# Expert results added to output rows by scattering transfers, in place of a slot store and a gather at the end

## The chip, the cores and the metric

The kernel runs on one core of a Trainium2 chip. The metric is device time in microseconds; the time before is the median of 3 runs, 1596.5 us (1591.99 to 1597.85). TensorE does the products, VectorE (DVE) and ScalarE (ACT) the elementwise work, GpSimd (POOL) elementwise work and the indirect DMAs, SyncE (SP) issues the plain DMAs.

## The reference

One layer on 1250 rows of 1024 features, in float32. Three parts follow one another: a graph convolution over 20000 edges and linear attention with 16 heads, both on the normalised rows and added to them, and then a mixture of 8 experts, 2 per row, whose result is added to the row:

```python
xn = _layernorm(x, axis=-1)
x = x + _L0_gnn_ref(xn, edge_index, L0_gnn_W, L0_gnn_b) + _L0_mix_ref(xn[None], ...)[0]
x = x + _L0_ffn_ref(_layernorm(x, axis=-1)[None], ...)[0]
...
logits = jnp.einsum('bsd,ed->bse', x, gate_w) + gate_b
topv, topi = jax.lax.top_k(logits, K)                       # K = 2 of E = 8
gate_score = jax.nn.softmax(where(keep > 0, logits, -inf))
expert_out = jnp.einsum('bsd,edo->bseo', x, expert_w) + expert_b
out = jnp.einsum('bseo,bse->bso', expert_out, gate_score)
```

## The kernel before

The change is in the third part and in the routing ahead of it. `x2` in SBUF holds the rows after the first two parts, ten tiles of 128 rows (TT = 10, the last of 98). Its normalised rows lie in DRAM in two halves of 512 columns, `x2n_half[c]`.

**Routing.** DVE finds the two best experts of each row (`choose`), makes the one-hot `both`, and TensorE counts rows per expert and ranks them (L1721 to L1726). DVE then works out for each row and choice its slot: every expert gets whole tiles of 128 slots, at least two, so that tile T of 128 slots belongs to one expert; `cnti` holds for each expert the number of tiles less one (`more`) and the first tile (`begin`). A product of `hotr` (which slot within a tile) and `hott` (which tile, times the row number), 20 matmuls (L1732), turns the table round: `slots[:, T]` is the row that each slot of tile T works on. The gate weights `gab` are worked out behind that, off any chain that waits for them (L1426 to L1435).

**Expert stage.** The tiles are worked through in order, in run-time loops (`experts`, `expert`, `tile_of`). For the given inputs these are 23 tiles, three to an expert and two for one. For tile T:

- POOL gathers its rows in two halves, `gather_tile`: a copy of the slot column to `here`, then an indirect DMA to `xg`.
- TensorE transposes a half (`transposes`, L1742), ACT makes the high part `mth` of it (`prepare`, L1054), DVE the low part `mtl` (`prepare`, L1391). This is done for tile T + 1 while tile T is multiplied: half 0 in the middle of tile T, half 1 at its end.
- TensorE multiplies in 48 matmuls of 512 columns (`tile`, L1756, L1757, L1759) in k order, k = 0 to 3 first, the transposes of the next tile, k = 4 to 7, the transposes again. Its results lie in one of two pairs of PSUM banks, by T odd or even, so `tile(T + 2)` waits for the copy of T.
- DVE adds the expert's bias `ebb` and copies to `ybuf` (`copy_out`, L1404), of which there is one, and SP stores it to its 128 slots in the DRAM tensor `slot_y` (`store_tile`, L590).

In the last tile of an expert ACT and DVE also split the next expert's weights into a high part (`high`, L1021) and a low part (L1419), k = 0 to 3 in the middle of the tile and k = 4 to 7 at its end; there `copy_out` comes behind those splits. SP loads the weights two experts ahead (`load_expert`, eight DMAs of 512 KB) once the last product of an expert is done, then stores that tile, then loads the next bias.

**Tail.** When all but the last expert's tiles are stored, POOL gathers for each of ten row tiles the result of its first choice (`gather_results`, L840), and when all tiles are stored those of the second. DVE multiplies each by its gate weight and adds it to `x2` (`combine`, L1444), and SP stores the finished row tiles to `out` (L615).

Engines run their own instruction streams, in the order written; everything between them goes by semaphores. SP's plain DMAs go through one queue, POOL's through another. To have no undefined numbers in slots that stay empty, SP fills `slot_y` with rows of x during attention (L527, 7 transfers).

Of the kernel before, what the change touches and what calls it, by code (L numbers as in the profile page):

```python
# [24 lines left out]
FILL = MAXT * P // (KT - 1)  # L25
assert FILL * (KT - 1) == MAXT * P and FILL <= NP
# [29 lines left out]
def gps_layer(nc, x, dst_pairs, src_cols, dst_cols, wg, bg, wq, bq, wk, bk, wv, bv, wo, bo, orf,  # L56
              gate_w, gate_b, expert_w, expert_b, out):
    x2n_half = [nc.dram_tensor(f"x2n_half{c}", [NP, CW], F32, kind="Internal").ap() for c in range(NC)]
    slot_y = nc.dram_tensor("slot_y", [MAXT * P, D], F32, kind="Internal").ap()
# [4 lines left out]
    with ctx:  # L64
# [49 lines left out]
        hott = keep("hott", [P, 2 * TT, MAXT], F32, s1)  # L114
# [103 lines left out]
        pc = ExitStack()  # L218
        gathered = keep("gathered", [P, 2 * KT, D], F32, pc)
        pc.close()  # L220
# [32 lines left out]
        pos = keep("pos", [P, 2, TT], I32)  # L253
        token = keep("token", [P, TT], F32)
# [5 lines left out]
        here = keep("here", [P, NC], I32)  # L260
        gw = keep("gw", [P, KT, E], F32)
# [107 lines left out]
        s_pos = sem("s_pos")  # L369
        slot_hot = sem("slot_hot")  # L370
        slots_filled = sem("slots_filled")
# [12 lines left out]
        y_stored = [sem(f"y_stored{c}") for c in range(NC)]  # L384
        z_stored = [sem(f"z_stored{c}") for c in range(NC)]
        a_gathered = sem("a_gathered")
        b_gathered = [sem(f"b_gathered{i}") for i in range(TT // 2)]
        comb_a = sem("comb_a")
        comb_b = sem("comb_b")
# [59 lines left out]
        def _(sp):  # L449
# [72 lines left out]
            with sp.Fori(1, KT) as j:  # L522
                for i, w in enumerate((wk, wv, wq)):

                    sp.wait_ge(a_w, START + 3 * j + i)
                    sp.dma_start(hraw[:, :, :], w[ds(j, 1)].rearrange("a p k n -> (a p) k n")).then_inc(a_raw, 16)
                sp.dma_start(slot_y[ds((j - 1) * FILL, FILL), :], x[0:FILL, :]).then_inc(slots_filled, 16)  # L527

# [57 lines left out]
            def store_tile(T, e, last):  # L586
                for c in range(NC):

                    sp.wait_ge(y_copied[c], T + 3)
                    sp.dma_start(slot_y[ds(T * P, P), c * CW:(c + 1) * CW],  # L590
                                 ybuf[:, c, :]).then_inc((z_stored if last else y_stored)[c], 16)

            def expert(e, par, last):
                more, begin = tiles(sp, e)
                with sp.Fori(0, more) as i:
                    store_tile(tile_of(begin + i), e, last)
# [5 lines left out]
                store_tile(T, e, last)  # L602
                if not last:

                    load_bias(e + 1)

            sp.wait_ge(slots_filled, 16 * (KT - 1))
            sp.wait_ge(s_cnti, 1)
            experts(sp, expert)


            for t in range(TT):
                n = LAST if t == TT - 1 else P
                sp.wait_ge(comb_b, t + 1)
                sp.dma_start(out[t * P:t * P + n, :], x2[0:n, t, :]).then_inc(s_out, 16)  # L615
# [4 lines left out]
        def _(pool):  # L620
# [31 lines left out]
            for signal in (rest_taken, rest_over, a_w, t_done, s_done, sq_ready, phi_done, kv_done, aux_done, kv_evac,  # L652
                           mt_trans, *y_stored, *z_stored):
# [128 lines left out]
            g.iota(token[:, :], [[P, TT]], base=0, channel_multiplier=1,  # L782
# [26 lines left out]
            def gather_tile(T):  # L809
                for c in range(NC):  # L810

                    pool.wait_ge(mt_trans, START + 2 * T - 1 + c if c else START + 2 * T - 1)
                    apart(pool)
                    g.tensor_copy(here[:, c:c + 1], slots[:, ds(T, 1)]).then_inc(here_ready, 1)
                    pool.wait_ge(here_ready, 2 * T + c + 1)
                    apart(pool)
                    g.indirect_dma_start(xg[:, c, :], None, x2n_half[c][:, :],
                                         bass.IndirectOffsetOnAxis(ap=here[:, c:c + 1], axis=0)).then_inc(xg_ready[c], 16)
# [24 lines left out]
            for t in range(TT):  # L843
                gather_results(t, 0, t, a_gathered)
# [984 lines left out]
```

## Time and profile before

| | |
|---|---|
| median of 3 runs | 1596.5 us |
| the profiled execution's own time | 1595.47 us |
| its span, first to last instruction | 1593.9 us |
| TensorE busy with matmuls | 1408.8 us (88%) |
| VectorE, ScalarE, GpSimd busy | 761.6, 465.5, 385.9 us |
| mean granted TensorE clock | 0.957 |

The span is that of one execution on the chip. A row of a timeline has the start, the duration, the engine (SPq is SyncE issuing), the line of the kernel, the operation and what it writes and reads, and in brackets how long the engine stood idle before it and what ended that. The busy share of an engine is a mean over stages with different limits, so a table by stage says more than the page's first lines.

### The profile page before, as it was taken

What the parts mean: (1) busy time and instruction counts of PE and PEld (TensorE: products, weight loads), DVE (VectorE), ACT (ScalarE), POOL (GpSimd) and SP (SyncE); (2) the same over time, 40 slices, a digit from 0 to 9 for tenths busy, and PEclk for the clock granted to TensorE, in tenths of its full rate; (3) what the DMA queues carried; (4) which work ended last, traced back from release to release, by engine and by line L of the source; (5) the groups of instructions that cost most, each with busy time, mean ns of one, the idle gap of its engine ahead of it and who ended that gap; (6) DMA issues with size and microseconds to landing.
All of it is one profiled execution on the core that took longest, in us unless ns stands there. A gap on an engine that the chain in (4) does not pass through costs nothing.

```text
span 1593.9 us, 26331 instructions
## 1 busy us (share of the span) xinstructions
PE 1408.8 (88%) x8396; PEld 1241.5 (78%) x8460; DVE 761.6 (48%) x1492; ACT 465.5 (29%) x777; POOL 385.9 (24%) x382
## 2 busy tenths in 40 slices
PE   5787778987889999999999999997999499999980
PEld 2465566887879999999999999996888388888860
DVE  7755443414354444444444444445454435444536
ACT  7412222401023232323333333332223023223310
POOL 7421443233230101010101010004034212122233
PEclk9999999998999999999999999998998599999995
DMA  4110111244321111111111101004234336665557
GB/s 152 52 36 17 60 46 71 73 134 127 96 87 73 39 67 37 69 40 66 40 66 43 63 33 59 1 1 140 77 128 145 126 96 239 237 237 201 215 205 280
DMA packets 64820, 158.19 MB, mean 99 GB/s; under 512 B 8010, under 2 KB 29210, under 8 KB 64320
## 3 DMA queue, kind: packets, MB, share of 16 engines
q1 hardware_dynamic: 55200, 127.20, 22.7%
q0 software_dynamic: 9568, 30.30, 6.1%
q8 instruction: 32, 0.52, 0.1%
q14 instruction: 20, 0.16, 0.0%
HBM read 120.05 MB, written 55.78 MB: 110 GB/s over the span
## 4 chain that ended last, share of the span: by engine, by line
PE 74%; DMA 8%; DVE 6%; issue 5%; POOL 2%; ACT 2%; DVEq 2%; SPq 1%; POOLq 0%; ACTq 0%
PE PB L1579 6%; PE PB L1581 6%; PE PB L1580 6%; DMA y_scratch<-xrow 5%; PE PB L1756 5%; PE PB L1757 5%; PE PB L1759 5%; PE PB L1615 5%; PE PB L1638 4%; PE PB L1481 4%; PE PB L1563 2%; PE PB L1565 2%; PE PB L1564 2%; PE PB L1522 2%; PE PB L1523 2%
## 5 line engine op out<-in xcount | busy, mean ns | idle before, releaser
L1579 PE MATMUL PB<-xh,hw 128*128 128x416 f32 (+1 forms) x576 | 205.0, 356 | 5.5 <-ACT qf L966 5.5
L1581 PE MATMUL PB<-xh,hw 128*128 128x416 f32 (+1 forms) x576 | 203.0, 352 | 0.0
L1580 PE MATMUL PB<-xl,hw 128*128 128x416 f32 (+1 forms) x576 | 202.8, 352 | 0.0
L1756 PE MATMUL PB<-mwh,mth 128*128 128x512 f32 x368 | 149.0, 405 | 1.3 <-issue 1.3
L1481 PE MATMUL PB<-ohs,ohd 128*128 x471 | 105.8, 346 | 48.8 <-DVE ohs L1127 32.6
L1757 PE MATMUL PB<-mwl,mth 128*128 128x512 f32 x368 | 144.5, 393 | 0.0
L705 POOL CAST hw<-hraw 128x1024 fp32r<-128x1024 f32 x24 | 24.9, 1037 | 455.5 <-PE PB L1581 450.7
L1481 PEld LDWEIGHTS PB<-ohs,ohd 128*128 x534 | 51.7, 97 | 101.5 <-issue 84.4
L1550 PE MATMUL PB<-hh,AT 128*128 128x256 f32 x400 | 103.7, 298 | 18.2 <-DVE hr L1141 9.2
L1579 PEld LDWEIGHTS PB<-xh,hw 128*128 128x128 f32 x576 | 108.6, 189 | 7.6 <-ACT qf L966 6.5
L1125 DVE TENSOR_SCALAR ohd<-iota,dc 128x128 f16 x178 | 60.0, 337 | 113.9 <-PE PB L1481 101.7
L1759 PE MATMUL PB<-mwh,mtl 128*128 128x512 f32 x368 | 114.2, 392 | 0.0
L1580 PEld LDWEIGHTS PB<-xl,hw 128*128 128x128 f32 x576 | 108.7, 189 | 1.2
L1581 PEld LDWEIGHTS PB<-xh,hw 128*128 128x128 f32 x576 | 108.6, 189 | 1.2
L1127 DVE TENSOR_SCALAR ohs<-iota,sc 128x1280 f16 x178 | 101.8, 572 | 0.0
L1551 PE MATMUL PB<-hr,AT 128*128 128x256 f32 x400 | 101.2, 292 | 0.0
L1550 PEld LDWEIGHTS PB<-hh,AT 128*128 128x128 f32 x400 | 80.5, 201 | 21.3 <-DVE xrow L1178 10.4
L1054 ACT ACTIVATE mth<-PB 128x512 fp32r<-128x512 f32 x48 | 28.7, 598 | 226.2 <-PE PB L1742 226.2
L1522 PE MATMUL PB<-wqh,xh 128*128 128x256 f32 x320 | 91.7, 287 | 3.1 <-DVE xl L1134 1.7
L1391 DVE TENSOR_TENSOR mtl<-PB,mth 128x512 fp32r<-128x512 f32 x48 | 33.0, 688 | 126.6 <-ACT mth L1054 126.6
L966 ACT ACTIVATE qf<-PB,biasT 128x416 f32<-128x416 f32 (+1 forms) x48 | 29.2, 609 | 216.3 <-PE PB L1581 167.2
L1523 PE MATMUL PB<-wql,xh 128*128 128x256 f32 x320 | 90.5, 283 | 0.0
(261 smaller groups left out, 3147.7 us busy)
## 6 DMA issues: line engine op xcount, KB each, us to landing
mraw<-expert_w SPq DMA_DIRECT2D x64, 512.0 KB, 7.5
slot_y<-x SPq DMA_DIRECT2D x7, 2560.0 KB, 12.1
slot_y<-ybuf SPq DMA_DIRECT2D x46, 256.0 KB, 3.4
count_rests<-ATf POOLq DMA_DIRECT2D x9, 640.0 KB, 3.3
xrow<-x SPq DMA_DIRECT2D x40, 128.0 KB, 2.4
y_scratch<-xrow SPq DMA_DIRECT2D x40, 128.0 KB, 2.4
yrow<-y_scratch SPq DMA_DIRECT2D x20, 256.0 KB, 2.9
x2n_half<-xhat SPq DMA_DIRECT2D x20, 256.0 KB, 2.5
```

What stands on the lines that cost most here:

```text
L1127: v.tensor_scalar(ohs[:, ds(2 * side + p, 1), :].rearrange("p a n -> p (a n)"), iota[:, :], sc[:, ds(col, 1)], None, ALU.is_equal).then_in ...
L1481: ins = mm(PB[:, 1536 * s + c0:1536 * s + c0 + n], ohd[:, ds(2 * side + p, 1), :].rearrange("p a n -> p (a n)"), ohs[:, ds(2 * side + p, 1 ...
L1522: mm(o, xh[:, k, at], wqh[q % 2][:, k, :], start=(k == 0), stop=False)
L1523: mm(o, xh[:, k, at], wql[q % 2][:, k, :], start=False, stop=False)
L1550: mm(o, AT[:, b, at], hh[:, q % 2, b, :], start=(b == 0), stop=False)
L1551: ins = mm(o, AT[:, b, at], hr[:, q % 2, b, :], start=False, stop=(b == TT - 1))
L1579: mm(bank(i, n), hw[:, wi, 0, k, :], xh[:, k, c0:c0 + n], start=(k == 0), stop=False)
L1580: mm(bank(i, n), hw[:, wi, 0, k, :], xl[:, k, c0:c0 + n], start=False, stop=False)
L1581: ins = mm(bank(i, n), hw[:, wi, 1, k, :], xh[:, k, c0:c0 + n], start=False, stop=(k == KT - 1))
L1756: mm(y[c], mth[:, k, :], mwh[par][:, k, c * CW:(c + 1) * CW], start=(k == 0), stop=False)
L1757: mm(y[c], mth[:, k, :], mwl[par][:, k, c * CW:(c + 1) * CW], start=False, stop=False)
L1759: ins = mm(y[c], mtl[:, k, :], mwh[par][:, k, c * CW:(c + 1) * CW], start=False, stop=(k == KT - 1))
```

## The change

The result of an expert tile is no longer stored by slots. At the start of the expert stage SP writes `x2` to `out`. For each tile DVE copies the products with the bias to `ybuf` as before, ACT multiplies both halves by the gate weight of each slot (`scale`), and POOL adds the 128 rows to their rows of `out` with one indirect DMA that accumulates in DRAM (`add_tile`); empty slots aim beyond the last row and are left out by the bounds check. `copy_out` of the next tile waits until that transfer has landed, which POOL waits for half a tile later (`tile_added`) and tells by `y_free`; the last one is awaited by SP. For this, routing turns two tables round instead of one: the slot's row number (for the gather, `slots`, and for the scatter, `target`) and its gate weight (`gate`), so `hott` is twice as wide and `gab` is worked out earlier, ahead of DVE's wait for TensorE's counts. In the last tile of an expert `copy_out` and `scale` stand ahead of the splits for k = 4 to 7; the last tile of all has no `prepare` behind it any more. `slot_y`, its fills, the gathers and the combines at the end are gone, and the stores of `out` are at the start.

```diff
+            for t in range(TT):
+                n = LAST if t == TT - 1 else P
+                sp.dma_start(out[t * P:t * P + n, :], x2[0:n, t, :]).then_inc(s_out, 16)
...
             def expert(e, par, last):
                 more, begin = tiles(sp, e)
-                with sp.Fori(0, more) as i:
-                    store_tile(tile_of(begin + i), e, last)
                 T = tile_of(begin + more)
                 if not (isinstance(e, int) and e >= E - 2):
                     sp.wait_ge(prod_done, T + 1)
                     load_expert(e + 2, par)
-                store_tile(T, e, last)
                 if not last:
+                    for c in range(NC):
+                        sp.wait_ge(y_copied[c], T + 3)
                     load_bias(e + 1)
...
+            more, begin = tiles(sp, E - 1)
+            sp.wait_ge(y_added, 16 * (begin + more + 1))
             sp.wait_ge(s_out, 16 * TT)
```

On POOL (`gather_half(T, c)` is one half of the old `gather_tile(T)`):

```diff
+            def aim(T):
+                g.tensor_copy(there[:, :], target[:, ds(T, 1)]).then_inc(there_ready, 1)
+            def add_tile(T):
+                pool.wait_ge(y_scaled, NC * (T + 1))
+                pool.wait_ge(there_ready, T + 1)
+                g.indirect_dma_start(out[:, :], bass.IndirectOffsetOnAxis(ap=there[:, 0:1], axis=0),
+                                     ybuf[:, :, :].rearrange("p c n -> p (c n)"), None, bounds_check=N - 1,
+                                     oob_is_err=False, compute_op=ALU.add).then_inc(y_added, 16)
+            def tile_added(T):
+                pool.wait_ge(y_added, 16 * (T + 1))
+                pool.sem_inc(y_free, 1)
+                aim(tile_of(T + 1))
...
-            with pool.Fori(0, begin + more + 1) as T:
-                gather_tile(tile_of(T + 1))
...
+            gather_half(1, 0)
+            gather_half(1, 1)
+            pool.wait_ge(targets_ready, 1)
+            aim(0)
+            gather_half(2, 0)
+            gather_half(2, 1)
+            pool.wait_ge(s_out, 16 * TT)
+            add_tile(0)
+            with pool.Fori(2, begin + more + 1) as T:
+                gather_half(tile_of(T + 1), 0)
+                tile_added(tile_of(T - 2))
+                gather_half(tile_of(T + 1), 1)
+                add_tile(tile_of(T - 1))
+            tile_added(tile_of(begin + more - 1))
+            add_tile(tile_of(begin + more))
```

On ACT and DVE:

```diff
+            def scale(T):
+                for c in range(NC):
+                    act.wait_ge(y_copied[c], T + 3)
+                    a.mul(ybuf[:, c, :], ybuf[:, c, :], gate[:, ds(T, 1)]).then_inc(y_scaled, 1)
             def expert(e, par, last):
                 with act.Fori(0, more) as i:
                     for h in range(2):
                         prepare(begin + i + 1, h)
-                for h in range(2):
-                    prepare(begin + more + 1, h)
-                    if not last:
+                    scale(tile_of(begin + i))
+                if not last:
+                    for h in range(2):
+                        prepare(begin + more + 1, h)
+                        if h == 1:
+                            scale(tile_of(begin + more))
                         for k in range(4 * h, 4 * h + 4):
                             high(e + 1, k, 1 - par)
+                else:
+                    scale(tile_of(begin + more))
...
             v.tensor_tensor(both[:, :, :], oneh[:, 0], oneh[:, 1], ALU.add).then_inc(s_both, 1)
+            dve.wait_ge(s_ge, 1)
+            link(v.tensor_scalar(gd[:, 3, :], gd[:, 1, :], 1.0, None, ALU.add))
...
             dve.wait_ge(route_done, 1)
...
-            for i in range(2):
-                v.tensor_tensor(hott[:, i * TT:(i + 1) * TT, :], hota[:, i * TT:(i + 1) * TT, :], token..., ALU.mult)
+            for i, value in enumerate((token[:, :], gab[:, 0, :, :].rearrange("p i t -> p (i t)"))):
+                v.tensor_tensor(hott[:, :, i, :], hota[:, :, :], along(value, MAXT), ALU.mult).then_inc(slot_hot, 1)
...
-                    if last:
-                        dve.wait_ge(y_stored[c], START + 16 * begin)
-                        dve.wait_ge(z_stored[c], START + 16 * i)
-                    else:
-                        dve.wait_ge(y_stored[c], START + 16 * T)
+                    dve.wait_ge(y_free, T + START)
...
-            v.tensor_copy(slots[:, :], bank(2, MAXT)).then_inc(slots_ready, 1)
+            v.tensor_scalar(slots[:, :], found[:, 0:MAXT], float(FAR), float(N - 1), ALU.add, ALU.min).then_inc(slots_ready, 1)
+            v.tensor_copy(gate[:, :], found[:, MAXT:2 * MAXT])
+            v.tensor_scalar(target[:, :], found[:, 0:MAXT], float(FAR), None, ALU.add).then_inc(targets_ready, 1)
```

On TensorE only the slot product changes, from `hott[0:n, i, :]` of MAXT = 35 columns to both tables, 70 columns.

## Rows read from the trace of the kernel before

**Rows 1.** Table by stage: busy of each engine, then PEclk, DMA share, GB/s.

```profile
1236.00:1269.00 33.00, 12.12 (x56) 11.79 (x55) 16.97 (x57) 0.21 (x1) 6.62 (x6) 0.50 0.37 136
1269.00:1547.70 278.70, 276.97 (x1296) 228.08 (x1296) 122.78 (x147) 81.17 (x103) 62.38 (x100) 0.99 0.56 197
```

**Rows 2.** Timeline of the tail: start, duration, engine, line, operation.

```profile
1546.69 0.62 PE L1759 MATMUL PB<-mwh,mtl 128*128 128x512 f32 x2
1549.10 1.28 DVE L1404 TENSOR_TENSOR ybuf<-PB,ebb 128x512 f32<-128x512 f32 x2
...
1558.55 1.18 POOL L840 DMA_INDIRECT gathered<-slot_y,pos  x1 [8.10 <-DMA slot_y<-ybuf]
...
1571.07 19.70 SPq L615 DMA_DIRECT2D out<-x  x10
```

**Rows 3.** Timeline of one tile within an expert.

```profile
1298.95 0.60 ACT L1054 ACTIVATE mth<-PB 128x512 fp32r<-128x512 f32 x1 [5.33 <-PE PB L1742]
...
1299.97 0.97 POOL L817 DMA_INDIRECT xg<-x2n_half,here  x1 [0.79 <-POOL here L814]
...
1304.15 0.60 PE L1742 MATMUL PB<-ident,xg 128*128 128x128 f32 x4
```

**Rows 4.** Landing times of transfers from `resty` (L726) and then to `gathered` (L840).

```profile
DMA to landing us min/median/max: 3.1/3.5/3.9
...
DMA to landing us min/median/max: 4.6/6.7/11.9
```

**Rows 5.** DMA queues and issues, windows 445.3:450, 319.9:324, 324:330, 1266:1270.5.

```profile
q0 software_dynamic: 288, 0.20, 33.0%
...
q0 software_dynamic: 144, 0.07, 8.8%
...
q1 hardware_dynamic: 576, 0.52, 27.6%
...
q0 software_dynamic: 160, 0.52, 41.8%
...
xg<-x2n_half,here POOLq DMA_INDIRECT x2, 3.5
```

**Rows 6.** Timeline of the routing stage, DVE and POOL.

```profile
1243.31 0.24 DVE L1350 COPY tot<-PB 128x80 f32<-128x80 f32 x1 [1.97 <-PE PB L1725]
...
1254.86 0.95 DVE L1385 TENSOR_TENSOR hott<-hota,token 128x350 f32<-128x350 f32 x2
...
1264.76 0.16 DVE L1427 TENSOR_SCALAR gd<-gd 128x10 f32<-128x10 f32 x1
...
1265.52 1.16 POOL L828 DMA_INDIRECT xg<-x2n_half,here  x1 [0.29 <-POOL here L825]
...
1266.86 0.17 DVE L1435 TENSOR_TENSOR gab<-gab 128x10 f32<-128x10 f32 x1
```

**Rows 7.** Groups by line and shape: busy us, mean ns of one, idle before.

```profile
L1732 PE MATMUL PB<-hott,hotr 128*128 128x35 f32 x36 | 8.1, 408 | 12.6 <-DVE hott L1385 12.6
...
L1724 PE MATMUL PB<-both,upper 128*128 128x72 f32 x2 | 0.7, 456 | 3.9 <-DVE both L1347 3.9
```

**Rows 8.** What the DMA engines moved in 1236:1265, in 40 slices.

```profile
GB/s 0 113 282 350 418 418 396 401 441 407 418 429 396 429 390 401 96 0 0 0 0 0 0 0 0 0 0 0 0 0 0 0 0 0 0 0 0 0 0 0
```

**Rows 9.** Timeline of a boundary of two experts, and the late bias.

```profile
1311.29 3.90 ACT L1021 ACTIVATE mwh<-mraw 128x1024 fp32r<-128x1024 f32 x4
1311.43 0.69 DVE L1391 TENSOR_TENSOR mtl<-PB,mth 128x512 fp32r<-128x512 f32 x1 [0.35 <-ACT mth L1054]
...
1312.38 4.63 DVE L1419 TENSOR_TENSOR mwl<-mraw,mwh 128x1024 fp32r<-128x1024 f32 x4 [0.26 <-ACT mwh L1021]
...
1316.01 0.60 PE L1742 MATMUL PB<-ident,xg 128*128 128x128 f32 x4
...
1328.32 1.29 DVE L1404 TENSOR_TENSOR ybuf<-PB,ebb 128x512 f32<-128x512 f32 x2 [4.34 <-DMA ebb<-expert_b]
```

**Rows 10.** Landing of xg in the window 1310:1330, with eight weight loads.

```profile
xg<-x2n_half,here POOLq DMA_INDIRECT x4, 5.9
```

More of the change, by code:

```diff
@@ L24 @@
 MAXT = (2 * N + 2 * (P - 1)) // P + 1 + 2 * (E - 2) + 1
-FILL = MAXT * P // (KT - 1)
-assert FILL * (KT - 1) == MAXT * P and FILL <= NP
+FAR = 4096
 CHUNKS = ((0, 512), (512, 512), (1024, NP - 1024))
@@ L260, in gps_layer @@
         here = keep("here", [P, NC], I32)
+        target = keep("target", [P, MAXT], I32)
+        there = keep("there", [P, 1], I32)
+        gate = keep("gate", [P, MAXT], F32)
         gw = keep("gw", [P, KT, E], F32)
@@ L383, in gps_layer @@
         y_copied = [sem(f"y_copied{c}") for c in range(NC)]
[L384 to L389, printed above, removed]
+        targets_ready = sem("targets_ready")
+        y_scaled = sem("y_scaled")
+        there_ready = sem("there_ready")
+        y_added = sem("y_added")
+        y_free = sem("y_free")
         s_out = sem("s_out")
@@ L807, in _, with gather_half @@
                 low(k)
[L809 to L818, printed above, removed]
+            def gather_half(T, c):
+                pool.wait_ge(mt_trans, START + 2 * T - 1 + c if c else START + 2 * T - 1)
+                apart(pool)
+                g.tensor_copy(here[:, c:c + 1], slots[:, ds(T, 1)]).then_inc(here_ready, 1)
+                pool.wait_ge(here_ready, 2 * T + c + 1)
+                apart(pool)
+                g.indirect_dma_start(xg[:, c, :], None, x2n_half[c][:, :],
+                                     bass.IndirectOffsetOnAxis(ap=here[:, c:c + 1], axis=0)).then_inc(xg_ready[c], 16)
             pool.wait_ge(slots_ready, 1)
@@ L829, in _ @@
                                      bass.IndirectOffsetOnAxis(ap=here[:, c:c + 1], axis=0)).then_inc(xg_ready[c], 16)
-            more, begin = tiles(pool, E - 1)
-            with pool.Fori(0, begin + more + 1) as T:
-                gather_tile(tile_of(T + 1))
-            for c in range(NC):
-                pool.wait_ge(y_stored[c], START + 16 * begin)
-                apart(pool)
-            def gather_results(t, i, at, done):
-                n = LAST if t == TT - 1 else P
-                g.indirect_dma_start(gathered[0:n, at, :], None, slot_y[:, :],
-                                     bass.IndirectOffsetOnAxis(ap=pos[0:n, i, t:t + 1], axis=0)).then_inc(done, 16)
@@ L843, in _ @@
[L843 to L854 removed]
+            def aim(T):
+                apart(pool)
+                g.tensor_copy(there[:, :], target[:, ds(T, 1)]).then_inc(there_ready, 1)
@@ L1392, in prepare, with copy_out @@
                                 mth[:, 4 * h:4 * h + 4, :].bitcast(F32), ALU.subtract).then_inc(mt_low, 1)
-            def copy_out(T, e, i, begin, last):
+            def copy_out(T, e):
                 for c in range(NC):
@@ L1411, in expert @@
                         prepare(begin + i + 1, h)
-                    copy_out(begin + i, e, i, begin, last)
-                for h in range(2):
-                    prepare(begin + more + 1, h)
-                    if not last:
+                    copy_out(begin + i, e)
+                if not last:
+                    for h in range(2):
+                        prepare(begin + more + 1, h)
+                        if h == 1:
+                            copy_out(begin + more, e)
                         for k in range(4 * h, 4 * h + 4):
```

77 lines of the change are left out of this document (20 added, 57 removed).

## Prediction

> **What bounds the kernel now.** I read the page first, for the order of the stages, then the table by stage, then the timelines where one stage turns into the next. The table puts numbers on it: from 1269 to 1547.7 us TensorE works 277.0 of 278.7 us at a granted clock of 0.99 (the 2.4 GHz level), while the 33 us of routing ahead of it run at 0.50 (1.2 GHz) with TensorE busy for 12 [rows 1]. The last product ends at 1546.69 + 0.62 = 1547.3 and the span at 1593.9, so 46.6 us hold no product at all [rows 2]. Three stages count, each with its own limit: routing is a chain of small DVE and TensorE steps, the expert stage is TensorE alone, the tail is transfers. What the change does in a stage has to be read against that stage's limit.
>
> **What goes: the tail.** After the last product come a copy, a store, ten gathers that waited 8.1 us for that store, combines behind the gathers, and ten output stores issued from 1571.07 to 1590.8 [rows 2]. All of that is replaced.
>
> **What comes in its place.** The last copy_out no longer stands behind a prepare, so its two halves (1.28 us [rows 2]) run from 1547.35 to 1548.65. ScalarE then scales the second half: no such instruction is in the trace; the nearest is the 128x512 ACTIVATE at 0.60 [rows 3]; end 1549.25. POOL waits and issues: the shortest gap ahead of an indirect issue is 0.29 [rows 6], the one behind a copy and its wait is 0.79 [rows 3]; I take 0.5, issue at 1549.75. Then the scattering transfer, X us from issue to landing, and 0.3 (a gap of that kind) until the span closes. The end is 1550.05 + X.
>
> **X, which the trace doesn't show.** From below: a gather of the same 128 rows of 4 KB landed in 4.6 at the quickest. The only accumulating transfers are the four of 128 KB in 1 KB rows, which landed in 3.1 to 3.9 [rows 4]. The queue shares tell what they cost the DMA engines. Queue 0 held 33.0% of 16 engines over 4.7 us (24.8 engine-us) for one such transfer and the load of restb in front of it; a load of restb alone held 8.8% over 4.1 us (5.8). That leaves 19.0 for 128 rows, 0.148 each. Plain 1 KB rows: 27.6% over 6 us is 26.5 for 512 rows, 0.052 each [rows 5]. An accumulated row costs 0.10 more, or 2.85 times as much. A gathered 4 KB of xg costs 41.8% of 4.5 us, 30.1 for 128, 0.235; eight rows per engine are then 2.65 us with the constant added and 5.4 with the factor. An xg gather of 3.5 us has 0.94 of data, so 2.6 of fixed time [rows 5], and X is 5.25 by the first and 8.0 by the second. The bounds are 4.6 and 8.0. I take 6.0, nearer to the additive reading, since the quick landings of 3.1 to 3.9 are mostly fixed time.
>
> By the Trainium skill, Collectives: The Full Stack, "The bandwidth ceiling: the fold count and why AG ≠ RS ≠ AR", an add in a DMA engine reads two sources for each write and so runs at half the rate of a copy. By that the data part is 3.8 (twice two xg gathers), X is 6.4, and the sum below would be 0.4 later. The trace's 1 KB rows are worse than a factor of two.
>
> The stage ends at 1556.05 if nothing ahead of it moves: 37.85 saved.
>
> **Routing, on the path.** Eleven small DVE links (1264.76 to 1267.03, 2.3 us) move between `both` and the wait for TensorE's counts. That wait was 1.97 long [rows 6] and ScalarE's exp comes before it, so 0.35 shows (bounds 0 and 2.3). The two `hott` products, 0.95 together [rows 6], double their columns: +0.8 (0.7 to 0.95); `pos` goes, less than 0.1, left out. The 40 slot matmuls get 70 columns for 35. At this same low clock 72 columns take 0.456 and 35 take 0.408, 48 ns [rows 7]; as those ends are modelled I take 0.03 each, 1.2 (bounds 0 and 1.9). Sum +2.35, less what `pos` gave: 2.25. The copies for `gate` and `target` come after slots_ready, under the first gather; POOL's `aim` lies ahead of a wait for TensorE.
>
> **Ten stores of x2 to out, earlier.** SyncE issues them behind expert 1's eight loads. Those moved at about 400 GB/s and were over at 1248 [rows 8]; 5.1 MB more at that rate end at 1261, and the first xg gather is issued at 1265.5 [rows 6]. Free; without that cover the first gather is late by some us. POOL's wait for them stands before add_tile(0), with gather_half(3, 0) behind it, all long after.
>
> **slot_y fills.** Seven transfers from DRAM to DRAM during attention go. POOL and TensorE wait for none of them: 0; a gain is excluded by TensorE's products bounding that stage.
>
> **Each tile in the expert stage.** A tile takes 11.86 us (transposes at 1304.15 and 1316.01 [rows 3, 9]). ybuf is single, and its ring is now copy 1.28, scale 0.6, POOL 0.5, X, release 0.3: 2.7 + X, 8.7 for X = 6. It fits while X is under 9.15. tile_added has the second gather_half queued behind it on POOL, whose rows TensorE wants a tile later; the wait on y_free has prepare of the next tile behind it on DVE, wanted at the end of that tile. ScalarE's 1.2 us more per tile lie in idle of 5.33 [rows 3]. All hidden under TensorE's products, and uncovered from 9.15 on.
>
> **The boundary of two experts** (seven). copy_out and scale move ahead of the weight splits for k = 4 to 7. Before: mtl ends at 1312.12, then four highs in 3.90 and four lows in 4.63. After: copies to 1313.4, scale to 1314.05, first high to 1315.1, first low (1.2) to 1316.3; TensorE wants it right after the transposes of 1316.01, at 1316.35 [rows 9]. The margin is nil. I charge 0.15 each, 1 us. SyncE asks for the bias sooner, no store being ahead of it, but behind the same 4.2 MB of loads, and the scatter takes more of the DMA engines than the store did; ebb arrived at 1328.3 [rows 9] and I leave it there.
>
> **Sum.** 1593.9 - 37.85 + 2.25 + 1.0 = 1559.3 of span; 1.57 us lie outside the span (1595.47 - 1593.9), so 1560.9. The profiled execution was 1.0 under the median of the runs, 1596.5. I predict 1561.5. Bounds: X -1.4 to +2, routing -1.5 to +2.9, boundaries -1 to +7: 1557.5 to 1573.5.
>
> **Rivals.** (1) *The boundaries stall.* While eight loads run, an xg gather lands in 5.9 instead of 3.5 [rows 5, 10]. A scatter of 8 undisturbed is then slower still, and takes 4 us more of the engines than the store did, so the bias comes later too. Worked out for the worst: first copy of an expert 1331, its scatter lands 1341.5; second copy 1342, landing 1352.5; the last tile's copy is wanted at 1347.7 and highs and lows wait behind it: 5 us at the six boundaries that follow a burst, 30, so 1590; a middle case is 1575. For it: the nil margin. Against it: with X = 6 the ring recovers within a tile. Chance 0.17.
>
> The Trainium skill, DMA: Bandwidth & Descriptors, "Queues, rings and completion order", has each engine take turns between the queues with work, packet by packet. The landings of xg in the burst agree. By that rule a scatter of 6 takes 9.4 there, just past the ring, and one of 8 takes 13.4, which is the worst case.
>
> (2) *The scatter is the bound: slower.* One mechanism: read, add and write of 4 KB rows take longer than a tile leaves. Each us of X above 9.15 costs 22 us over 23 tiles. At X = 10.7 the gain is gone, from 11.1 the kernel is slower by over 0.5%, and X = 12 gives 1561.5 + 22 x 2.85 = 1624. For it: the factor of 2.85, and gathers and loads on the same engines. Against it: even the factor gives 8.0 undisturbed. Chance 0.10.
>
> (3) *The x2 stores reach into the first gather, or an indirect issue blocks on POOL while its queue is full*: the gain shrinks by 10 to 25 us, 1572 to 1586. Chance 0.08.
>
> The forecast holds the remaining 0.65. Range: 1555 to 1584. A measurement of this kernel tells about 0.5% (8 us) from nothing. Faster by more 0.87, within it 0.04, slower 0.09.
>
> **What the new profile would show.** The last scatter landing in 5 to 8 us and the span ending 8 to 11 us after the last product; slots at 1266 to 1268; slot matmuls near 10 us; TensorE idle in the expert stage at most 5 us more, tiles still 11.86 apart; the stores of x2 over before the first xg. I am wrong if DVE waits for y_free at every tile, or TensorE for mwl at the boundaries.

## The result, and the profile after

The changed kernel took 1572.8 us (median of four runs, 1569.7 to 1575.4) against 1595.2 for the kernel before on the same chip: a ratio of 0.986, 95% interval 0.9832 to 0.9887. The forecast was 1561.5, within 1555 to 1584. The gain is real and 11 us smaller than forecast. The profiled execution (1575.38, span 1573.8) stands beside the 1593.9 of before, 20.1 us less. The same table by stage as [rows 1], with the tail as a third window:

```profile
1236.00:1271.20 35.20, 14.13 (x64) 13.74 (x64) 17.16 (x58) 1.92 (x3) 7.40 (x7) 0.50 0.73 274
1271.20:1560.80 289.60, 281.08 (x1296) 230.03 (x1296) 124.02 (x147) 108.25 (x146) 105.66 (x137) 0.98 0.61 177
1560.80:1573.80 13.00, 0.00 (x0) 0.00 (x0) 1.07 (x2) 1.33 (x2) 1.62 (x1) 0.64 0.11 16
```

TensorE's last product now ends 13.4 us before the span does, where it was 46.6 [rows 2]. But the expert stage, 278.7 us long before, is 289.6 for the same 1296 instructions. A good part of what the tail gave was lost there.

**The tail**, in the timeline of all engines, and below it SyncE's and GpSimd's closing instructions (the last two columns of each are nanoseconds and the first and last start):

```profile
1559.74 0.62 PE L1750 MATMUL PB<-mwh,mtl 128*128 128x512 f32 x2
...
1560.58 1.29 DVE L1412 TENSOR_TENSOR ybuf<-PB,ebb 128x512 f32<-128x512 f32 x2 [9.00 <-PE PB L1750]
1561.47 1.33 ACT L1055 ACTIVATE ybuf<-ybuf,gate 128x512 f32<-128x512 f32 x2 [8.94 <-DVE ybuf L1412]
1563.93 1.62 POOL L823 DMA_INDIRECT out<-ybuf,there  x1 [3.39 <-issue]
```
```profile
L62 POOLq DRAIN  x1: 9912/9912/9912, 1563.7 to 1563.7; - x1
L62 SPq COMPARE_BRANCH  x1: 38/38/38, 1569.9 to 1569.9; - x1
```

SyncE is released at 1569.9, so the last scatter landed 5.9 us after its issue; the forecast had 6.0. The agreement is partly luck: this scatter moved 0.21 MB, since most slots of the last tile are empty (the one before it, 0.52 MB, landed in 6.6), and the others outside a burst of weight loads landed in 6.0 to 6.6. GpSimd's closing drain, which begins with that issue, ends at 1563.7 + 9.9 = 1573.6, and the span with it.

**The expert stage.** The transposes that end each half of a tile were 5.93 us apart before (1280.44 to 1547.14 in 45 steps). I call what is over 45 such steps (266.7 us) the losses. The third transposes and the last ones now:

```profile
1283.59 0.60 PE L1733 MATMUL PB<-ident,xg 128*128 128x128 f32 x4
...
1560.20 0.60 PE L1733 MATMUL PB<-ident,xg 128*128 128x128 f32 x4
```

1560.20 - 1283.59 - 266.7 = 9.9 us of losses, where before had none. They are not spread evenly: five places, each near a boundary of experts, hold 9.2 of them (1.7, 0.7, 1.4, then 3.9 and 1.5 about the expert of two tiles). The waits that go with them, from the list of waits (engine, tile and line, what released it: us in all, times, the longest):

```profile
POOL there L816 <- DMA out<-ybuf,there: 72.6, 22, 5.7
...
DVE ybuf L1412 <- DMA ebb<-expert_b: 25.2, 6, 5.4
...
DVE ybuf L1412 <- POOLq L830: 14.2, 9, 3.1
...
PE PB L1733 <- DMA xg<-x2n_half,here: 8.6, 3, 4.6
...
PE PB L1747 <- DVE mwl L1429: 2.8, 3, 1.3
```

DVE's wait for the bias is nearly as large as before, when it was 29.0 us in six. New are the nine waits for y_free (released by POOLq L830). Of TensorE's 8.6 us for xg, 4.8 lie ahead of the first tile's products (bias_pair, which loses next to nothing, has them too), and one wait of 3.8 is in the stage. Its three waits "for mwl" need care, since the list names the releaser that came last before the wait ended. The first of these places is in the timeline:

```profile
1332.64 1.29 DVE L1412 TENSOR_TENSOR ybuf<-PB,ebb 128x512 f32<-128x512 f32 x2 [5.36 <-DMA ebb<-expert_b]
...
1335.81 1.61 POOL L823 DMA_INDIRECT out<-ybuf,there  x1 [5.25 <-ACT ybuf L1055]
...
1342.21 0.18 POOL L816 COPY there<-target 128x1 int32 x1 [2.81 <-DMA out<-ybuf,there]
...
1343.32 0.96 POOL L801 DMA_INDIRECT xg<-x2n_half,here  x1 [0.79 <-POOL here L798]
...
1345.42 1.62 POOL L823 DMA_INDIRECT out<-ybuf,there  x1 [1.14 <-ACT ybuf L1055]
...
1345.93 4.63 DVE L1429 TENSOR_TENSOR mwl<-mraw,mwh 128x1024 fp32r<-128x1024 f32 x4 [0.26 <-ACT mwh L1015]
...
1348.95 0.60 PE L1733 MATMUL PB<-ident,xg 128*128 128x128 f32 x4
...
1350.80 0.49 PE L1747 MATMUL PB<-mwh,mth 128*128 128x512 f32 x1 [1.25 <-DVE mwl L1429]
```

The list's reading, late splits for k = 0 to 3, doesn't fit. The product at 1350.80 needs the low part for k = 0 alone, the first of the four, and that ended at 1345.93 + 1.23 = 1347.16; the 1350.56 that the list goes by is the end of the fourth. What fits is TensorE's own instruction stream. At the start of an expert it reads the expert's number of tiles and first tile from `cnti` in SBUF (L395, L396), as it does in every kernel here; the column PEldq is its sequencer, the numbers are nanoseconds (min/median/max). These are the two reads at this place, then all eight of L396 in the changed kernel and in bias_pair:

```profile
L395 PEldq TENSOR_LOAD <-cnti x1: 596/596/596, 1347.5 to 1347.5; - x1
L396 PEldq TENSOR_LOAD <-cnti x1: 1147/1147/1147, 1348.6 to 1348.6; - x1
...
L396 PEldq TENSOR_LOAD <-cnti x8: 297/722/1535, 1273.8 to 1522.9; - x8
...
L396 PEldq TENSOR_LOAD <-cnti x8: 296/302/309, 1274.2 to 1514.2; - x8
```

So read it as this chain. The bias of the new expert lands behind eight weight loads, so the expert's first copy_out runs at 1332.64. Its scatter is issued at 1335.81 and holds ybuf for 6.4 us. The second tile's copy_out waits until 1342.24. GpSimd too waits for that landing, until 1342.21, so the gather_half behind it is issued at 1343.32 and lands at 1346.57. TensorE's stream, which otherwise runs ahead of its products, waits for that xg and comes to the two reads at 1347.47, 1.5 us ahead of the transposes, where bias_pair has 2.4. There they meet the next late scatter (issued at 1345.42) and take 0.60 and 1.15 us instead of 0.30 each. The second ends at 1349.72 and the product starts 1.08 later, where it would have followed the transposes at 1349.30. At the two other places (0.7 and 1.4 us) the product starts 1.13 and 1.12 us after the second read too, and 3.4 and 3.6 us after the low part that it needs. The three together are 3.7 us.

About the expert of two tiles the late scatter (1480.64) stands directly in front of a gather_half, and TensorE waits for its xg:

```profile
1480.64 1.61 POOL L823 DMA_INDIRECT out<-ybuf,there  x1 [5.37 <-ACT ybuf L1055]
1481.67 1.88 POOL L798 COPY here<-slots 128x1 int32 x1
1484.34 1.20 POOL L801 DMA_INDIRECT xg<-x2n_half,here  x1 [0.79 <-POOL here L798]
...
1493.12 1.09 PE L1733 MATMUL PB<-ident,xg 128*128 128x128 f32 x4 [3.77 <-DMA xg<-x2n_half,here]
```

In bias_pair that gather is issued 4.1 us ahead of the previous transposes, here 1.1 us behind them, and it lands in 8.5 us, with the next eight weight loads issued from 1483.61 on. The 1.5 us that follow are TensorE's clock. After these 3.8 us without products the granted clock was 0.50 (the 1.2 GHz level) for 3.4 us, and a product took 0.63 us for 0.39:

```profile
1493.00:1496.20 3.20, 3.08 (x10) 2.63 (x11) 2.65 (x3) 0.81 (x2) 0.96 (x2) 0.50 1.03 334
```

The same kernel's other trace, changed_again, has its 9.0 us in part elsewhere: 4.1 at the same three places and 0.9 by two waits for xg at others, but 1.65 and 1.58 where the low part for k = 4 does come too late, since the tile's copy_out ahead of it had waited for y_free:

```profile
1490.99 3.50 DVE L1429 TENSOR_TENSOR mwl<-mraw,mwh 128x1024 fp32r<-128x1024 f32 x3 [1.92 <-ACT mwh L1015]
...
1492.36 0.47 PE L1747 MATMUL PB<-mwh,mth 128*128 128x512 f32 x1 [1.41 <-DVE mwl L1429]
```

Its first low part ends at 1492.22. So a late scatter is common to all these places, and by which way it reaches TensorE changes from place to place and from run to run.

**Routing** cost less than forecast. From the timeline of DVE and the groups by shape:

```profile
1244.85 0.24 DVE L1365 COPY tot<-PB 128x80 f32<-128x80 f32 x1
...
1256.32 0.89 DVE L1399 TENSOR_TENSOR hott<-hota,token 128x700 f32<-128x700 f32 x1
1257.12 0.88 DVE L1399 TENSOR_TENSOR hott<-hota,gab 128x700 f32<-128x700 f32 x1
```
```profile
L1722 PE MATMUL PB<-hott,hotr 128*128 128x70 f32 x36 | 8.2, 423 | 13.5 <-DVE hott L1399 13.5
```

The eleven links moved `tot` 0.25 us back (2.46 us behind the start of `both`, 2.21 before). The x2 stores, with expert 1's loads, filled the DMA engines until about 1262, and the first xg was issued at 1267.8. They cost nothing.

### The profile page after: what moved, and what is told of

Same layout as the page of the kernel before. It is cut to its first block, busy times and chain, and to the rows that moved or that the text cites. A ratio compares the mean times of both kernels' runs of the same rounds, so it can differ in the third digit from the quotient of the medians.

```text
span 1573.8 us, 26445 instructions
## 1 busy us (share of the span) xinstructions
PE 1428.5 (91%) x8459; PEld 1245.6 (79%) x8460; DVE 735.5 (47%) x1471; ACT 493.4 (31%) x821; POOL 411.1 (26%) x408
## 3 DMA queue, kind: packets, MB, share of 16 engines
q1 hardware_dynamic: 48016, 96.79, 17.8%
## 4 chain that ended last, share of the span: by engine, by line
PE 72%; DMA 12%; DVE 5%; issue 5%; ACT 2%; SPq 2%; POOL 1%; DVEq 0%; POOLq 0%; ACTq 0%
PE PB L1569 7%; PE PB L1571 7%; PE PB L1570 7%; PE PB L1471 6%; DMA y_scratch<-xrow 6%; PE PB L1605 5%; PE PB L1628 4%; PE PB L1747 4%; PE PB L1748 3%; PE PB L1750 3%; DMA ebb<-expert_b 2%; PE PB L1553 2%; PE PB L1555 2%; PE PB L1554 2%; PE PB L1512 2%
## 5 line engine op out<-in xcount | busy, mean ns | idle before, releaser
L1471 PE MATMUL PB<-ohs,ohd 128*128 x534 | 120.3, 352 | 36.9 <-issue 23.3
L1130 DVE TENSOR_SCALAR ohd<-iota,dc 128x128 f16 x178 | 55.1, 309 | 115.4 <-PE PB L1471 104.7
L1132 DVE TENSOR_SCALAR ohs<-iota,sc 128x1280 f16 x178 | 106.8, 600 | 0.0
L1514 PE MATMUL PB<-wqh,xl 128*128 128x256 f32 x320 | 90.5, 283 | 0.0
L1747 PEld LDWEIGHTS PB<-mwh,mth 128*128 128x128 f32 x368 | 70.3, 191 | 19.2 <-issue 5.5
```

Of the source, the lines that this page charges most:

```text
L1132: v.tensor_scalar(ohs[:, ds(2 * side + p, 1), :].rearrange("p a n -> p (a n)"), iota[:, :], sc[:, ds(col, 1)], None, ALU.is_equal).then_in ...
L1471: ins = mm(PB[:, 1536 * s + c0:1536 * s + c0 + n], ohd[:, ds(2 * side + p, 1), :].rearrange("p a n -> p (a n)"), ohs[:, ds(2 * side + p, 1 ...
L1747: mm(y[c], mth[:, k, :], mwh[par][:, k, c * CW:(c + 1) * CW], start=(k == 0), stop=False)
```

## The experiments

Theory A for the losses changed on the way. In the first expectations (bias_pair, copy_behind_splits, scatter_without_add) it is the late bias that costs, and the ring of ybuf only hands the delay on. After their results it has two conditions: the bias is late, *and* the single ybuf is held until its slow, adding scatter lands. The main rivals, by the letters of the expectations below: the scatter alone is too slow (B of bias_pair), the late bias alone is enough (D of scale_on_gpsimd), the place of the copies costs (C) or doesn't matter at all (G), or GpSimd has too much to do (E of scale_on_gpsimd). The letters B, D and E stand for other things in other expectations. The table has all runs; "losses" and "tail" (from the start of the weight loads of the last transposes to the end of the span) are worked out from the traces in one way for all.

```
run                             time us   ratio (95%)              losses  tail
before                          1595 to 1598                        0.0    47.0
the changed kernel              1572.8    0.986  (0.983 to 0.989)    9.9    13.8
changed_again                   1576.4    0.988  (0.986 to 0.990)    9.0    14.1
bias_pair                       1564.6    0.980  (0.977 to 0.983)    1.4    14.6
bias_pair_again                 1567.0    0.981  (0.979 to 0.984)    1.4    14.3
bias_ahead_of_weights           1568.6    0.982  (0.979 to 0.985)    2.0    14.1
scatter_without_add (1 run)     1560.8                               1.7    12.5
copy_behind_splits              1575.3    0.987  (0.984 to 0.990)    9.5    14.4
bias_pair_copy_behind_splits    1573.3    0.986  (0.983 to 0.988)   11.8    14.4
scale_on_gpsimd                 1616.6    1.014  (1.010 to 1.017)   46.2    20.5
scale_on_gpsimd_bias_pair       1618.2    1.013  (1.009 to 1.016)   48.3    21.1
last_by_plain_store (1 run)     1568.9                               9.1     7.8
gpsimd_waits_for_last_landing   1570.7    0.984  (0.982 to 0.986)    1.4    17.8
```

**bias_pair.** The bias of an expert is loaded two experts ahead, into one of two buffers (and the semaphores of biases and raw weights are split by parity).

```diff
-        ebb = keep("ebb", [P, D], F32)
+        ebb = keep("ebb", [P, 2, D], F32)
...
-            load_bias(0)
+            load_bias(0, 0)
+            load_bias(1, 1)
...
-                if not last:
...
-                    load_bias(e + 1)
+                    load_bias(e + 2, par)
```

> Edit: two bias buffers, the bias of an expert loaded two experts ahead (and semaphores for weights and bias kept apart by parity); nothing else. In the changed kernel VectorE waited 25.2 us in all for ebb, 14.2 for y_free, and TensorE lost 9.9 us against an even 5.93 us per half tile. Theory A (the late bias starts the delays, the ring of ybuf only hands them on): waits for ebb below 2 us, waits for y_free below 5, TensorE's losses below 3, time about 8 us less, 1565. Rival B (the scattering transfer is too slow for the ring by itself while the weights load): waits for ebb gone, but 10 us and more for y_free, losses of 6 to 9, time 1570 or more.

Losses fell from 9.9 to 1.4 us, with no wait for ebb left and 5.8 us for y_free (just over the 5 expected), and so the scatter alone (B) is not enough:

```profile
  PE PB L1750: 9.0, 1
  POOLq L830: 5.8, 5
```

The stretch of the expert stage, with TensorE busy for 279.0 of 280.9 us, is within 2.2 us of what it was in [rows 1]:

```profile
1271.60:1552.50 280.90, 279.00 (x1296) 228.83 (x1296) 123.30 (x147) 109.25 (x146) 103.22 (x137) 0.98 0.63 181
```

**bias_ahead_of_weights.** One buffer, but SyncE issues the bias first (the semaphores of the raw weights are split by parity as in bias_pair).

```diff
                     sp.wait_ge(prod_done, T + 1)
-                    load_expert(e + 2, par)
+                    apart(sp)
                 if not last:
...
                     load_bias(e + 1)
+                if not (isinstance(e, int) and e >= E - 2):
+                    load_expert(e + 2, par)
```

> SyncE issues the next expert's bias ahead of the eight 512 KB weight loads instead of behind them; the buffer stays single. SyncE therefore also waits for the tile's two copies (y_copied) before it issues the weights. Theory A (the bias is late because it queues behind eight weight loads, and the late copy is what the single ybuf and its scatter turn into a TensorE wait): ebb lands in 3 to 5 us instead of 13.6, DVE waits for ebb fall from 25.2 to below 5, waits for y_free from 14.2 to about the 5.8 of the run with the pair of biases, expert-stage losses below 3 us, time 1563 to 1568. Rival B (the weights, issued some 2 us later, become late instead): ACT's splits wait for mraw, losses stay, time 1570 or more.

No wait for ebb is left, y_free 8.8 us, losses 2.0. Its time, 1568.6, is just over the range given. Rival B of this run falls: the weights, asked for later, were not missed. The order of two requests on SyncE's queue is worth about 8 of the 9.9 us.

**scatter_without_add.** The scatter overwrites its rows instead of adding to them, so the sum over a token's two experts and its x2 is left out. The bias stays late.

```diff
-                                     oob_is_err=False, compute_op=ALU.add).then_inc(y_added, 16)
+                                     oob_is_err=False).then_inc(y_added, 16)
```

> Leaves out the addition: the scattering transfers overwrite the rows of out instead of adding to them, all else the same. It prices the add. The adding transfer landed in 6.5 us (median) and took 46.4% of 7.6 us of 16 engines, 56.4 engine-us for 128 rows, 0.44 each. Additive theory: a plain scattered row costs 0.10 less than an adding one, landing 5.9. Factor theory: a plain row costs a half or less, 0.15 to 0.22, landing 4.6 to 5.1. TensorE's losses: by theory A still 6 or more, because the bias stays behind 4.2 MB of loads; by rival B below 4.

Theory A missed here: it gave losses of 6 or more, and they are 1.7. DVE waits for the bias as long as ever, so the late bias alone, as A had it first and D has it later, is not enough. The buffer comes free sooner:

```profile
DVE ybuf L1412 <- DMA ebb<-expert_b: 25.3, 6, 5.2
```
```profile
1330.73 1.01 POOL L823 DMA_INDIRECT out<-ybuf,there  x1 [6.50 <-ACT ybuf L1055]
...
1334.40 0.19 POOL L816 COPY there<-target 128x1 int32 x1 [0.69 <-DMA out<-ybuf,there]
1334.43 1.29 DVE L1412 TENSOR_TENSOR ybuf<-PB,ebb 128x512 f32<-128x512 f32 x2 [0.26 <-POOLq L830]
```

The hold is 3.7 us instead of 6.4, and the waits for y_free fall from 14.2 us to 0.3. So neither condition costs by itself, and both together cost about 8 us. That the second condition is the hold of ybuf is argued, not shown: the edit takes more away than that. The scatter also takes less of the DMA engines, GpSimd issues it in 1.0 us for 1.6, and 15 of TensorE's 16 reads of `cnti` take 0.30 to 0.32 us, the other 0.58. (Of the 14.5 us by which its span is shorter than the changed kernel's, 8.2 are losses and 1.3 the tail. 3.5 were there before its first transposes and 1.5 come from its first tile at the low clock; in both the edit has no part.)

**copy_behind_splits** and **bias_pair_copy_behind_splits.** copy_out and scale of an expert's last tile stand behind all eight weight splits, as copy_out did before, with the single bias and with the pair.

```diff
                     for h in range(2):
                         prepare(begin + more + 1, h)
-                        if h == 1:
-                            copy_out(begin + more, e)
...
+                copy_out(begin + more, e)
```

> Edit: at the boundary of two experts copy_out and scale stand behind the weight splits for k = 4 to 7 again, as in the kernel before. My forecast saw the danger in that order (nil margin, 0.15 us each). If it is that, the small losses in the second half of the first tile after a boundary (0.17, 0.17, 0.36 us and the like) vanish and the time falls by 1 us. Theory A: the big losses (1.7, 0.7, 1.4, 3.9, 1.5) stay, since they come from the first tile's late bias; total 8 to 12, time 1571 to 1576. Rival C (the order is what costs): losses below 5, time 1568 or less.

> The pair of biases, and the tile's copy and scaling behind the eight weight splits, as the kernel before had them. Theory A (the late scatter, whatever makes it late, costs through ybuf and through GpSimd's gather queued behind it): the copies wait for y_free about 40 us in all as in the run with the copy behind the splits and the single bias, expert-stage losses 8 to 10 us, time 1571 to 1576, so moving the copies ahead of the last four splits is worth 7 to 10 us once the bias is there in time. Rival G (the place of the copies does not matter, only the bias does): 1563 to 1567.

Alone it changes nothing in the time, and that theory A's figure (8 to 12 us of losses) came out was luck. A gave them to the late bias, but the bias is then rarely waited for (4.7 us), while y_free is, 40.9 us in all. The copies come late because they stand behind the splits, and each late scatter reaches the next. TensorE loses most of it otherwise too, by six waits for xg of 6.5 us in all. With the pair it is 8.6 us slower than the pair alone, and DVE waits 44.7 us for y_free (of its losses 1.6 stand in 3.4 us at a granted clock of 0.50, from 1336.1 on). So the scatters about a boundary must be early, and two things make them late: the place of the last tile's copy and the bias of the next expert's first. Either spoils what curing the other would give, which is why the move in the changed kernel by itself showed no gain. Rivals C and G fall.

**scale_on_gpsimd** and **scale_on_gpsimd_bias_pair.** DVE's copy goes to a buffer of its own and GpSimd multiplies by the gate into ybuf; this was meant to take the hold of the scatter off DVE.

```diff
+                for c in range(NC):
+                    pool.wait_ge(y_copied[c], T + 3)
+                    g.tensor_scalar(ybuf[:, c, :], ypre[:, c * CW:(c + 1) * CW], gnow[:, 0:1], None,
+                                    ALU.mult).then_inc(y_scaled, 1)
```

> GpSimd multiplies by the gate just before its scatter, from a buffer of its own that DVE fills, so DVE's copy no longer waits for a landing and ScalarE no longer scales; the bias keeps its single buffer and its place. Theory A (two conditions together cost the 9.9 us: a late bias and a single result buffer held until the scatter lands): waits for y_free are gone, ebb waits stay near 25, expert-stage losses below 3 us as in the run without the addition (1.7), tail about 1 us longer by two GpSimd products of 0.5 to 1 us each in place of ScalarE's; time 1565 to 1569. Rival D (it is the late bias alone that costs, by holding DVE in front of the splits): losses stay 8 to 10, time 1573 or more. Rival E (GpSimd, now with 2 more us a tile, issues the gathers late): TensorE waits for xg, over 1575.

> Both at once: GpSimd scales from a buffer of its own, and the biases have a pair of buffers. Theory A: the losses were already down to 1.4 us with the pair of biases alone, so nothing more is to be had in the expert stage; the tail is up to 1 us longer; time 1564 to 1567, the same as with the pair alone (1564.6). Rival F (the five waits for y_free of 5.8 us that the pair of biases left still cost): 1561 to 1563.

Both miss theory A by some 50 us. Rival E holds, and I had underpriced it. A product took 1.7 us on GpSimd where ScalarE took 0.7, and a round of GpSimd (two products, scatter, landing, two gathers) passes a tile's 11.86 us: here 14.2 from one copy of `there` to the next, 1301.22 to 1315.40.

```profile
1301.22 0.18 POOL L819 COPY there<-target 128x1 int32 x1 [3.02 <-DMA out<-ybuf,there]
...
1303.42 3.15 POOL L828 TENSOR_SCALAR ybuf<-x,gnow 128x512 f32<-128x512 f32 x2
1307.49 2.69 POOL L832 DMA_INDIRECT out<-ybuf,there  x1 [0.91 <-POOL ybuf L828]
...
1315.40 1.20 POOL L819 COPY there<-target 128x1 int32 x1 [2.43 <-DMA out<-ybuf,there]
```

After the first tile TensorE waited 31.4 and 36.6 us for xg. As tests of theory A these two are void, since another engine became the bound. A pair of ybufs with everything else alike, which would test the hold itself, was not tried.

**last_by_plain_store.** The last tile's scatter is left out; SyncE stores its ybuf to the first rows of out in its place.

> Leaves out the last scatter: the last tile's scaled result goes to rows 0 to 127 of out by one plain store of SyncE. It asks what ends the span. In the changed kernel the last scatter landed 5.9 us after its issue, and the span ended 3.7 us later, with GpSimd's closing drain. Theory D (the drain ends 3.7 us after the last of GpSimd's own transfers has landed): the scatter before landed 0.1 us after the last product, so the drain ends 4 us after it, the store at about 6; the span ends 6 to 7 us after the last transposes begin instead of 13.6. Rival E (the drain takes about 10 us from where GpSimd's stream ends, whatever is in flight): 10 to 11 us after them.

The tail shrank by 6.0 us, to 7.8. The store was issued at 1562.44, SyncE was released at 1565.1 and the span ended 2.2 us later, with GpSimd's drain, although GpSimd had nothing outstanding:

```profile
L62 POOLq DRAIN  x1: 7427/7427/7427, 1559.7 to 1559.7; - x1
```

Both theories of this expectation miss. D had the drain end 3.7 us after the scatter before had landed (1559.56), and it took 7.4; E had about 10. The tail, 7.8, lies between the two.

**gpsimd_waits_for_last_landing.** bias_pair, and GpSimd waits for its own last landing before it ends.

```diff
             add_tile(tile_of(begin + more))
+            pool.wait_ge(y_added, 16 * (begin + more + 1))
```

> The kernel with the pair of biases, in which GpSimd itself waits for the landing of its last scatter before it comes to its end. In the runs so far GpSimd's closing drain began when the last scatter was issued and ended 3.7 us after that scatter landed; where the last tile left by SyncE (last_by_plain_store), GpSimd had already waited for everything and its drain still took 7.4 us. Theory H (a closing drain of GpSimd takes 7.4 us from its start and at least 3.7 us from the last landing, so the end of the program is GpSimd's whoever waits for the landing): the drain begins at the landing, takes 7.4 us, and the span ends some 18 us after the last transposes instead of 14.6; time about 1568, 3 to 4 us more than the 1564.6 of the pair alone. Rival I (the 3.7 us are only the last transfer's bookkeeping, done once it has landed): the drain takes 3.7 us or less from the landing and the time stays at 1563 to 1566.

```profile
L62 POOLq DRAIN  x1: 7059/7059/7059, 1559.6 to 1559.6; - x1
```

The drain began at the landing and took 7.1 us; the tail grew from 14.6 to 17.8. Theory H holds in the trace. The time, 1570.7, is 2.7 over what it gave (the ratio is 0.4 points above bias_pair's, some 7 us, of which the tail explains 3.3; the rest I can't place, as it isn't in this trace).

**bias_pair_again** and **changed_again**, five rounds each on one chip.

> The same kernel as bias_pair, timed in five rounds beside the changed kernel on one chip. Expected from the traces: 8 to 9 us below the changed kernel (expert-stage losses of 1.4 us in place of 9.9), ratio to the kernel before near 0.980.

> The changed kernel itself, unaltered, on the same chip as bias_pair_again: ratio to the kernel before near 0.986, and in its trace again waits of DVE for ebb near 25 us, for y_free near 14 us, and losses of 8 to 11 us in the expert stage.

9.4 us apart, with losses of 1.4 and 9.0 and waits for y_free of 6.1 and 17.7 us. The version with the pair of biases beats both kernels: 1.9% below before and 0.6% below the change, and its interval (0.979 to 0.984) lies clear of the change's (0.986 to 0.990).

## Why the prediction was right, and where it was off

The sum gave a span of 1559.3; it was 1573.8. By terms:

- **Tail, -37.85 forecast, -33.2 measured.** The mechanism was right, and X came out (5.9 for 6.0) on a last tile that is mostly empty. The step that failed is the last one, "0.3 until the span closes": it took 3.9, from GpSimd's drain (+3.6). The gap ahead of the issue was 1.13 for my 0.5, and scale ended 0.5 later, since ScalarE takes 0.7 a half and waits for each. Before, GpSimd's drain took 16.7 us and ended at 1591.4, 3.7 after its last gather had landed, and SyncE waited for the output stores until 1593.5, which hid it; the change took that cover away. I had read SyncE's end of the program as the program's end.
- **Boundaries, +1 forecast, +9.9 measured.** The largest miss. "Against it: with X = 6 the ring recovers within a tile" is the step that failed: the ring recovers, but only by delaying what stands behind it, GpSimd's next gather and DVE's next splits, and those have too little slack in an expert of three tiles. It was rival 1 (chance 0.17), at a third of the worst case's price and near its middle case (1575), to which the measured 1572.8 is nearer than to the 1561.5 forecast. But rival 1 had only its chain by the splits for k = 4 to 7. In the changed kernel's first trace that way cost some 0.6 us; the rest went by the gathers: 3.7 by TensorE's reads of `cnti`, 3.9 by the wait for xg, 1.5 by the low clock after it. In changed_again rival 1's own way took 3.2 of 9.0. The nil margin alone, on which I had charged the 1 us, cost 0.16 to 0.34 at each of the seven boundaries in bias_pair, 1.4 in all. Of the signs of being wrong, TensorE's wait for mwl at the boundaries came true in changed_again, and DVE waited for y_free in nine of 23 tiles.
- **Routing, +2.25 forecast, +0.3 measured** (1237.60 to 1264.65 before, 1239.56 to 1266.90 now). The 70 columns cost the slot matmuls 423 ns for 408, some 0.6 us over 40, and their stretch 0.1; the eleven links cost 0.25 for the 0.35 forecast; `hott` took 1.77 for 0.95, as forecast, and the first gd subtraction happened to take 0.7 less.
- **Free, as forecast:** the x2 stores, the slot_y fills, ScalarE's scaling inside an expert.
- **Not the change's:** +1.96 stood ahead of the routing stage, and +0.9 in the first tile, at the lower clock.

With these, -33.2 + 9.9 + 0.3 + 1.96 + 0.9 = -20.1, which is the difference of the spans. The measurement lies within the range, but the two large errors have the same sign: the range held them because it had room for rival 1. Rivals 2 and 3 fell: the scatter is far from bounding a tile, though its hold of ybuf took enough of a tile that one late bias used up the rest. The scatters' landings in the burst went as the Trainium skill's rule of turns between queues (DMA: Bandwidth & Descriptors, "Queues, rings and completion order") had them: by it 6 becomes 9.4 there, and the scatter issued at 1318.35, just behind the eight loads of 1313.6 to 1318.2, landed in 9.8, where the median of all was 6.5. The prediction says that the xg landings agreed as well, and that is too strong: its 2.6 fixed and twice 0.94 give 4.5, and they took 5.9.

## What to carry to other kernels

A wait that was harmless (25 to 29 us of DVE for a late bias, before and after) becomes costly when the change puts a longer hold behind it: price each old wait again with the new consumer at its end. When a transfer ends on a buffer with no second copy, follow the latest producer of that buffer through two rounds of the ring, not one, on every engine that waits for it. When a list says what a wait was for, check the time of the one result that the next instruction needs: here it had been there for over 3 us, and the engine's own instruction stream was late. And at the end of a program look at every engine's last instruction, not only at the one that waits for the output.

## What the runs showed of the hardware

- GpSimd's closing drain took 7.1 and 7.4 us even when all its transfers had landed; where the last one was still under way it ended 3.7 us after the landing (the changed kernel, bias_pair). In scatter_without_add it ended 5.2 us after the landing and 8.8 after its start. One reading fits all of these: 7.1 to 7.5 us from where GpSimd has nothing left to do (the drain's start, or the end of its last issue where that is later, 1551.55 in scatter_without_add), and at least 3.7 from the last landing. No run took the transfers off GpSimd altogether.
- An added row is dearer than forecast, and a plain one cheaper. The next to last scatter of the changed kernel, alone in 1553.4:1561, held 46.4% of 16 engines over 7.6 us: 56.4 engine-us for 128 rows, 0.44 each. In scatter_without_add the same one, in 1540.2:1545, held 27.6% over 4.8 us: 21.2, or 0.165 each.

```profile
q0 software_dynamic: 146, 0.52, 46.4%
```
```profile
q0 software_dynamic: 147, 0.53, 27.6%
```

So the addition makes a written row 2.66 times as dear, near the 2.85 that the 1 KB rows gave, and the additive reading (+0.10 a row for +0.275) fell, though X came out where it put it: 56.4 / 16 = 3.5 us of data and the 2.6 of fixed time give 6.1, since a scattered row starts from less than the 0.235 of a gathered one. The Trainium skill's half rate for an add (Collectives: The Full Stack, "The bandwidth ceiling: the fold count and why AG ≠ RS ≠ AR"), which the page has for the reduce-scatter of a ring of cores, is too cheap here: by it the 128 rows would take an estimated 42 engine-us, twice the plain 21.2.
- GpSimd's own time to issue the scatter is 1.62 us with the addition and 1.01 without.
- TensorE's stream reads a number from SBUF in 0.30 us. In all runs with the adding scatter, each read that began 2.0 to 4.2 us after the issue of an adding scatter took 0.41 to 1.53 us. GpSimd's copy of 128 slot numbers, 0.18 us, took 0.78 to 1.88 in the changed kernel when it began 1.0 us after that issue. Without that scatter a longer read came once each in scatter_without_add (0.58) and in the kernel before (0.80). What these reads share with the scatter is open.
